# Decoded weights and half of the norm rows turned in 32x32 blocks on VectorE in place of TensorE

## What is computed

```python
x = x + attention(layernorm(x), ctx, ctx, mask, wq, wk, wv, wo)   # 32 query heads, 8 key heads, rope
x = x + (layernorm(x) @ w_l.T + bias)     # w_l[o, i] = lut4[o, 4-bit code of (o, i)]
```

## Time and profile before

| what | us |
|---|---|
| median of 3 runs (2350.05 to 2352.4) | 2351.77 |
| span of the profiled execution, first to last instruction | 2348.6 |
| stage A / B / C in it | 384.3 / 1781.9 / 182.4 |
| TensorE busy | 2330.7 |
| VectorE busy | 1690.5 |
| ScalarE busy | 1115.5 |

### The profile page before, as it was taken

One profiled execution on the slowest core, in us unless ns is written; L12 is line 12 of the kernel. 1 busy time (PEld: TensorE's weight loads), 2 busy tenths in 40 slices (PEclk: granted clock), 3 DMA queues, 4 the chain that ended last, 5 costly groups with the idle time before them and its releaser, 6 DMA issues.

```text
span 2348.6 us, 35132 instructions
## 1 busy us (share of the span) xinstructions
PE 2330.7 (99%) x11878; PEld 1989.3 (85%) x11878; DVE 1690.5 (72%) x3808; ACT 1115.5 (47%) x2469; POOL 570.1 (24%) x674
## 2 busy tenths in 40 slices
PE   9999999999999999999999999999999999999999
PEld 8999998788888888888888888888888888888787
DVE  7888777677776767777776767676777777776773
ACT  5555544555464646455544445444544444443110
POOL 1000001222232223232322232223323232322220
PEclk9999999999999999999999999999999999999999
DMA  7466558533344343434457633333333333335442
GB/s 258 159 199 213 190 177 299 170 109 117 115 133 120 109 127 111 129 107 128 117 162 238 209 104 115 90 112 109 112 93 113 105 100 111 107 93 185 122 142 81
DMA packets 330098, 328.26 MB, mean 140 GB/s; under 512 B 32448, under 2 KB 266176, under 8 KB 329920
## 3 DMA queue, kind: packets, MB, share of 16 engines
q1 hardware_dynamic: 294496, 309.88, 42.8%
q10 hardware_dynamic: 35424, 16.14, 2.6%
HBM read 181.73 MB, written 71.30 MB: 108 GB/s over the span
## 4 chain that ended last, share of the span: by engine, by line
PE 92%; DVE 3%; DMA 3%; ACT 1%; SPq 1%; issue 1%; POOL 0%; ACTq 0%; DVEq 0%
PE bank L829 28%; PE bank L915 28%; PE bank L845 7%; PE bank L886 7%; PE bank L783 7%; PE bank L955 7%; PE bank L760 7%; DMA small_split<-probs 1%; DMA k_scratch<-small_split 1%; SPq L615 0%; POOL probs L1930 0%; DMA small_split<-k_scratch 0%; DVE residual L1804 0%; PE bank L721 0%; PE bank L741 0%
## 5 line engine op out<-in xcount | busy, mean ns | idle before, releaser
L915 PE MATMUL bank<-weights_split,small_split 128*128 128x512 f32 x3072 | 741.0, 390 | 1.9 <-DVE small_split L1788 1.9
L829 PE MATMUL bank<-acts_split,weights_split 128*128 128x512 f32 (+1 forms) x3168 | 742.9, 384 | 0.0
L915 PEld LDWEIGHTS bank<-weights_split,small_split 128*128 128x128 f32 x3072 | 574.4, 188 | 121.6 <-DVE small_split L1788 3.2
L829 PEld LDWEIGHTS bank<-acts_split,weights_split 128*128 128x128 f32 x3168 | 575.1, 188 | 110.6
L1930 POOL TENSOR_SCALAR probs<-probs,row_numbers 128x256 f32<-128x256 f32 x512 | 359.3, 714 | 1192.9 <-DVE row_numbers L1774 1192.9
L1248 ACT ACTIVATE probs<-bank,row_numbers 128x256 f32<-128x256 f32 x512 | 238.1, 472 | 125.2 <-DVE row_numbers L1769 125.0
L1778 DVE STREAM_TRANSPOSE probs<-probs 128x512 f32<-128x512 f32 x250 | 177.7, 711 | 145.2 <-POOL probs L1930 145.2
L1922 POOL TENSOR_TENSOR rope_x<-rope_x,sin_t 128x512 f32<-128x512 f32 (+1 forms) x132 | 166.7, 1263 | 404.7 <-ACT rope_x L1221 404.5
L1763 DVE CUSTOM_DVE_ANT_0 bank<-bank,mask_tile 128x256 f32<-128x256 f32 x512 | 207.2, 447 | 64.5 <-PE bank L845 64.4
L1783 DVE TENSOR_TENSOR small_split<-small_split 128x512 fp32r<-128x512 f32 x250 | 178.8, 715 | 85.2 <-ACT small_split L1261 85.0
L845 PEld LDWEIGHTS bank<-small_split 128*128 128x128 f32 x1536 | 217.6, 190 | 23.0 <-DVE small_split L1743 1.6
(11 more groups left out here) (124 smaller groups left out, 2167.0 us busy)
## 6 DMA issues: line engine op xcount, KB each, us to landing
small_split<-probs SPq DMA_DIRECT2D x754, 64.0 KB, 2.2
raw<-in_L_xattn_wq SPq DMA_DIRECT2D x61, 512.0 KB, 3.8
raw<-in_L_xattn_wo SPq DMA_DIRECT2D x60, 512.0 KB, 3.8
k_scratch<-small_split SPq DMA_DIRECT2D x64, 256.0 KB, 2.3
v_scratch<-small_split SPq DMA_DIRECT2D x32, 512.0 KB, 2.9
x_scratch<-raw SPq DMA_DIRECT2D x64, 256.0 KB, 2.8
acts_split<-x_scratch SPq DMA_DIRECT2D x32, 512.0 KB, 5.0
mask_tile<-in_mask_BxSxS_ff SPq DMA_DIRECT2D x64, 256.0 KB, 3.0
```

What stands on the lines that cost most here:

```text
L829: last = pe.matmul(query_bank(j)[:, 0:wide], wq_s[:, h, c, a, :], xT[:, c, m, b * S:b * S + wide], start=c == 0 and i == 0, stop=c == C - ...
L915: last = pe.matmul(out_ps[part][:, :], o_s[:, a, u % 2 * S + t * P:u % 2 * S + (t + 1) * P], wo_s[:, h, m, n * BANK:(n + 1) * BANK], start ...
```

## The change

Weight tiles 0 to 7 and row tiles 0 to 7 are turned by VectorE, with two STREAM_TRANSPOSE instructions of 128x512 each, from SBUF into the same PSUM banks as before. They turn each 32x32 block in itself. To make that enough, they read every fourth number of a row (`block_order`), and four DMAs of 32 partitions by 1024 numbers each (`store_blocks`) lay the blocks in DRAM so that it holds the picture of SBUF, which is then loaded in whole stripes of 4 KB (rows) or 8 KB (weights) per partition. The layouts of `w4_s`, `xT` (rows 0 to 7, `xT_blocks`) and `wv_s` follow; the moving operand of the queries of the first half and of stage C is then 16 runs of 32 numbers, 1 KB apart, where it was one run of 512. HI and LO of a tile now use one buffer one after the other: HI of both halves, four stores, then LO in its place once these have landed, four stores. Row tile 8 stays on TensorE, as do tiles 9 to 15 in stage B.

The first tile of stage C multiplies column half 0 fully and then half 1, because the pieces of `w4_s` are now halves of columns and parts; the turning of row tile 1 stands within it. The queries of batches 0 and 4 wait for all eight pieces of their `xT` half before the first one, not pair by pair.

The core of the diff:

```diff
         wk_s = W[:, :].rearrange("p (c l n) -> p c l n", c=C, l=2)
-        wv_s = X[:, :].rearrange("p (c l n) -> p c l n", c=C, l=2)
+        wv_s = X[:, :].rearrange("p (h c l n) -> p h c l n", h=NN, c=C, l=2)
...
         xT = X[:, :].rearrange("p (c l n) -> p c l n", c=C, l=2)
+        xT_half = X[:, :].rearrange("p (h c l n) -> p h c l n", h=2, c=C, l=2)
+        xT_blocks = X[:, :].rearrange("p (h l m c t) -> p h l c m t", h=2, l=2, c=C, t=QUAD)
...
-        w4_s = W[:, :].rearrange("p (c l n) -> p c l n", c=C, l=2)
+        w4_s = W[:, :].rearrange("p (h l m c t) -> p h l c m t", h=NN, l=2, c=C, t=QUAD)
...
+        def weight_stage(tile, part):
+
+            if tile == NB - 1:
+                return acc[:, HT - 2 + part, :].bitcast(F32R)
+            return x_split_all if tile == NB - 2 else v_stage_all
+
+        def block_order(row, half):
+
+            return row.rearrange("p (c i m) -> p m c i", c=C, i=QUAD)[:, 2 * half:2 * half + 2]
...
+            def store_blocks(image, at, src, done):
+
+                for a in range(PARTS):
+                    sp.dma_start(image[:, at + a * S:at + (a + 1) * S], src[a * QUAD:(a + 1) * QUAD, :]).then_inc(done, 16)
+
             def store_row(e, j):
 
+                if e < HT:
+                    if j == HI:
+                        sp.wait_ge(x_hi, 2 * e + 2)
+                    else:
+                        sp.wait_ge(x_lo, 2 * e + 2)
+                    store_blocks(x_blocks, (e // REP * 2 + j) * REP * D + e % REP * D, raw, x_stored)
+                    return
...
-                def store_weights(tile, i):
-                    sp.wait_ge(stage_lo, STAGED // 2 + staged_count(tile, i))
-                    stage, stored = staging(tile, i)
-                    dst = w_scr.rearrange("p j k (t n) -> t j p k n", n=P)
-                    sp.dma_start(dst[tile, i - D0], stage.bitcast(F32).rearrange("p (k n) -> p k n", n=P)
-                                 ).then_inc(stored, 16)
+                def store_weights(tile, part):
+                    sp.wait_ge(w4_lo if part else w4_hi, 2 * tile + 2)
+                    store_blocks(w_scr, (tile // REP * 2 + part) * REP * D + tile % REP * D,
+                                 weight_stage(tile, part).bitcast(F32), w4_stored)
...
-            def turn_weights(tile):
-
-                pe.wait_ge(w4_ready, tile + 1)
-                pe.wait_ge(stage_lo, STAGED // 2 + tile * STAGED)
-                for c in range(C):
-                    done = pe.transpose(w4_ps[c // 4][:, (c % 4) * P:(c % 4 + 1) * P],
-                                        picks[0][:, c * P:(c + 1) * P], ident[:, :])
-                    if c % 4 == 3:
-                        done.then_inc(w4_tr, 1)
...
                 values(0)
-                if b in K_ROW:
+                if b in K_ROW and K_ROW[b] >= HT:
                     turn_row(K_ROW[b])
                 values(1)
                 values(2)
                 values(3)
-                if b in V_ROW:
-                    turn_row(V_ROW[b])
...
-                columns = [(n, c) for n in range(NN) for c in range(C)] if f == NT - 1 else [
-                    (n, c) for c in range(C) for n in range(NN)]
-                for n, c in columns:
-                    if f == 0 and n == 0:
-                        pe.wait_ge(w4_in[c], 16)
-                    for i, (a, m) in enumerate(PASSES):
-                        last = pe.matmul(out_ps[f % 2 * NN + n][:, :],
-                                         xT[:, c, a, f % HT * P:(f % HT + 1) * P],
-                                         w4_s[:, c, m, n * BANK:(n + 1) * BANK],
-                                         start=c == 0 and i == 0, stop=c == C - 1 and i == 2)
-                    if c == C - 1:
+                if f == 0:
+                    products = [(0, c, k) for c in range(C) for k in range(3)]
+                    products += [(1, c, k) for c in range(C) for k in (0, 2)] + [(1, c, 1) for c in range(C)]
+                elif f == NT - 1:
+                    products = [(n, c, k) for n in range(NN) for c in range(C) for k in range(3)]
+                else:
+                    products = [(n, c, k) for c in range(C) for n in range(NN) for k in range(3)]
+                ends = [max(at for at, product in enumerate(products) if product[0] == n) for n in range(NN)]
...
+                    if f == 0 and (n, c, k) == (1, C // 2 - 1, 2) and PE_ROWS > 1:
+                        turn_rows(1)
...
+            def blocks_high(e):
+
+                act.wait_ge(x_tr, 2 * e + 2)
+                act.wait_ge(x_stored, rows_stored(e))
+                for j in range(2):
+                    act.activation(x_split[:, j, :], x_ps[j][:, :], ACT.Copy).then_inc(x_hi, 1)
...
+                def weights_high(tile):
+                    act.wait_ge(w4_tr, 2 * tile + 2)
+                    if tile == NB - 2:
+                        act.wait_ge(x_stored, rows_stored(A_ROWS))
+                    elif tile < NB - 2:
+                        act.wait_ge(v_stored, 16 * (v_turn(tile, V2) + 2))
+                    for j in range(2):
+                        act.activation(weight_stage(tile, HI)[:, j * BANK:(j + 1) * BANK], w4_ps[j][:, :],
+                                       ACT.Copy).then_inc(w4_hi, 1)
...
+            def turn_row_blocks_early(e):
+
+                dve.wait_ge(row_ok, e + 1)
+                dve.wait_ge(x_lo, 2 * e)
+                for j in range(2):
+                    dve.transpose(x_ps[j][:, :], block_order(ln_row[:, :], j)).then_inc(x_tr, 1)
+
+            def blocks_low(e):
+
+                dve.wait_ge(x_hi, 2 * e + 2)
+                dve.wait_ge(x_stored, rows_stored(e) + 16 * PARTS)
+                for j in range(2):
+                    dve.tensor_tensor(x_split[:, j, :], x_ps[j][:, :], x_split[:, j, :].bitcast(F32),
+                                      ALU.subtract).then_inc(x_lo, 1)
...
+            def turn_weight_blocks(tile):
+
+                dve.wait_ge(w4_ready, tile + 1)
+                dve.wait_ge(w4_lo, 2 * tile)
+                for j in range(2):
+                    dve.transpose(w4_ps[j][:, :], block_order(picks[0], j)).then_inc(w4_tr, 1)
+
+            def weights_low(tile):
+
+                dve.wait_ge(w4_hi, 2 * tile + 2)
+                if tile < NB - 1:
+                    dve.wait_ge(w4_stored, 16 * PARTS * (2 * tile + 1))
+                for j in range(2):
+                    half = slice(j * BANK, (j + 1) * BANK)
+                    dve.tensor_tensor(weight_stage(tile, LO)[:, half], w4_ps[j][:, :],
+                                      weight_stage(tile, HI)[:, half].bitcast(F32), ALU.subtract).then_inc(w4_lo, 1)
...
-                    if g == TURN_AT[b]:
-                        weights_low(b - 1, D0)
+                    if g == TURN_AT[b] - 1:
+                        turn_weight_blocks(b - 1)
                     if g == SECOND_AT[b]:
-                        weights_low(b - 1, D1)
...
+                if b in K_ROW and K_ROW[b] < HT:
+                    turn_row_blocks_early(K_ROW[b])
                 values_low(V0)
...
+                if b in K_ROW and K_ROW[b] < HT:
+                    blocks_low(K_ROW[b])
+                elif b in K_ROW:
                     x_low(K_ROW[b], 1, x_ps[1])
...
                 values_low(V2)
                 for j in range(4):
                     context_low(4 * (b + 1), j)
+                if b in V_ROW:
+                    turn_row_blocks_early(V_ROW[b])
```

181 lines of the change are left out of this document (83 added, 98 removed).

## The result

| | median us | runs | ratio to before, 95% interval |
|---|---|---|---|
| before | 2351.23 | 4 (2350.05 to 2352.4) | |
| changed kernel | 2394.47 | 4 (2392.12 to 2396.2) | 1.0179 (1.0165 to 1.0193) |

What follows compares the result with a forecast made beforehand. TensorE bounds the kernel, unless VectorE is late. Span 2348.6 - 3.6 (batches 1 to 7) + 0.3 (stage B) + 1.8 (stage C) = 2347.1; median 3.2 above: 2350.3 us; bounds 2347 to 2355.5, wider range 2342 to 2358.

Steps and rivals of the forecast that it cites:

- Bound and places: Whole kernel: TensorE bounds it; it would wait for VectorE ahead of V2 in batch 1 and behind V3 in 2 to 4.
- The image wait in batch 1: Batch 1: VectorE waits 1.2 us for the HI image's four stores, since HI and LO share a buffer.
- Stage C's step: Stage C: row tile 1 is turned behind 32 matmuls, not 24, and nothing covers the delay: +1.8 us.
- I take no cost: First-half queries and stage C: reading 16 runs of 32 costs TensorE nothing, from 394 ns against 390.
- I take no surcharge: VectorE's added transposes: reading every fourth number costs nothing extra, so a pair takes about 1.25 us.
- rival 4: First-half queries and stage C: short runs make 2304 matmuls 5 ns longer each, +11.5 us, 2361.8; chance 0.05.
- rival 3: VectorE's transposes at 16-byte steps: a pair takes 2.4 us, not 1.25; 12 pass on 1.15 each, +13.8, 2364; chance 0.06.
- the batches' terms: Stage A, batches 1 to 7: turns saved on TensorE less VectorE's lateness, together -3.6 us.
- term +1.4: Batch 1: V2 starts at 92.45 in place of 91.08, 1.4 us longer although 1.6 of TensorE work has gone.
- terms +1.1, -1.25, -1.25: Batches 2 to 4: batch 2 longer by the second row tile's later load and chain; 3 and 4 save 2.4 us, lose some.
- terms -3.6 together: Batches 5 to 7: mostly turns saved on TensorE, -1.2, -0.8 and -1.6 us.
- term +0.3: Stage B's start: all eight `xT` loads must land before the first queries; later idle time takes up most of it.

Runs made afterwards that it cites:

- e8_quarter: Kernel before, with 14 of the 16 turns that the change removes making two of their eight matmuls (results meaningless): 2347.28 us against 2352.29, ratio 0.9985.
- e12_quarter_again: The kernel of e8_quarter run once more, for a second trace: 2350.38 us.
- e4_plain: Changed kernel, with first-half queries and stage C reading one run of 512 and the 32 transposes reading one run (results meaningless): 2363.36 us.
- e1_reads: Kernel before, with stage C's moving operand read in another pattern of run length and step in most row tiles (results meaningless): 2368.41 us.
- e11_steps: Kernel before, with more moving-operand patterns in stage C and extra VectorE transposes and a copy at longer steps: 2359.08 us.
- e6_own_low: The kernel of e4_plain, with LO parts written to a spare buffer, so VectorE doesn't wait for the HI image (results meaningless): 2360.83 us.
- e10_turn12: Kernel before, complete, with row tile 1 turned behind the first 12 matmuls of stage C in place of 24: 2348.04 us against 2350.85, ratio 0.9986.
- e13_fill: Changed kernel, complete, with 57 more unread matmuls that keep TensorE busy in stage A's waits: 2392.94 us.
- e9_turn24: The kernel of e4_plain, with row tile 1 in stage C turned behind 24 matmuls again, not 32: 2363.97 us.
- cross of four kernels: Changed kernel with short runs or one run of 512, transposes reading every fourth number or one run: 2394.47, 2376.07, 2384.98, 2363.36 us.
- e5_turn_only: Changed kernel, with only the 32 transposes reading one run of 512 in place of every fourth number (results meaningless): 2384.98 us.

## Why the prediction was wrong, by its steps

**Bound and places: right.** TensorE waits where the text said: V2 of batch 1 behind V0's LO part, key 0 of batches 3 to 5 behind the context's. The turn is worth about what I took, 0.79 us: 14 times three quarters of a turn gave 8.3 us in stage A of e8_quarter and 6.6 in e12_quarter_again (0.63 each). The image wait in batch 1 was 1.14 us for 1.2. Stage C's step cost what it should: the wait was 4.03 us in e4_plain where it had been 2.28, 1.75 more for the forecast 1.8 (and the clock behind it came on top).

**The first step that failed: two terms of the sum put at nothing, "I take no cost" for the short runs and "I take no surcharge" for the transposes.** They stood as rivals 4 and 3, at chances of 0.05 and 0.06. Both were true at once and cost about 31 us, most of the 36 by which the time lies above my range. In both I let one row decide that didn't show the operation.

- *Short runs (rival 4).* The earlier trace rows showed 394 ns for runs of 64 against 390, and I explained the 4 ns away by what stands around line 886. By e1_reads runs of 64 cost 3 ns and runs of 32 ten to eleven. The row had the warning in it; the nearest pattern in the trace was twice as long as the new one, which is a reason to extrapolate beyond it. The rival's price should have been 4 to 10 ns on 2304 matmuls, 9 to 23 us, with a chance near one half. And the order of magnitude was at hand: a turn saves 0.79 us once, a turned weight tile is read by 96 matmul-shares (768 / 8) and a row tile by 192 (1536 / 8), so at 9 to 11 ns they cost 1.1 and 1.7 us each. The change could not gain on TensorE itself.
- *The transposes' step (rival 3).* I held L1459, 1264 ns for 1024 numbers at 128 bytes, against the contiguous transpose, 1246, and read "no surcharge". These are two operations. The copy in e11_steps with a step of 128 bytes takes 1.12 us per 512 against 0.69 for one run. L1459 is a TENSOR_SCALAR, and the one of that kind and size that reads one run in the kernel before (L1562, on integers) takes 819:

```profile
L1459 DVE TENSOR_SCALAR ln_row<-residual,row_numbers 128x1024 f32<-128x1024 f32 x16 | 20.3, 1267 | 27.7 <-DMA raw<-ln_row 27.6
...
L1562 DVE TENSOR_SCALAR residual<-residual,probs 128x1024 int32<-128x1024 int32 x64 | 50.8, 819 | 1.1 <-ACT residual L1113 1.1
```

So the surcharge was most likely in the row that I took as proof of its absence. The rule of the Trainium skill (page "SBUF — State Buffer", section "Door 1: The DMA port swizzle"), which spoke against the change, deserved more than 0.06. The surcharge was 0.7 to 0.8 us per pair, not the 1.15 of the rival, and it cost 11 us.

**The second: the batches' terms, even at my own prices.** In e4_plain batches 1 to 7 took 8.1 us more than in the kernel before (391.3 - 54.0 against 384.3 - 55.1), where the sum had -3.6. Batch 0, which had no term, was 1.1 shorter.

- *Batch 1*, term +1.4, measured +3.4 (50.28 for 46.89). V2 waited 3.56 us for 2.95, and 48 matmuls behind it took 12.63 us for 11.07: the clock, which no term had.
- *Batches 2 to 4*, terms +1.1, -1.25, -1.25, measured +3.2, +1.7 and +2.6. The row chain is longer than I made it. I took 10.0 us from the arrival of the second row to the context's LO part, less 1.2 us of waits that I thought gone. They are not. In e4_plain these steps of batch 2 take 10.0 us (144.11 to 154.13), and the load goes out 35.3 us into the batch for my 34.4: 1.2 + 0.9, the 2.1 by which the term was short. With the slower transposes it is more. In batch 2 of the changed kernel (ScalarE):

```profile
147.41 1.06 ACT L1025 ACTIVATE ln_row<-ln_row 128x1024 f32<-128x1024 f32 x1 [3.54 <-DMA ln_row<-in_x]
...
152.93 0.60 ACT L1040 ACTIVATE bank<-ln_row 128x512 f32<-128x512 f32 x1 [2.85 <-DVE raw L1445]
```

The load goes out 36.8 us into the batch, at 142.79, and takes 4.6 us, as I took it. But the squares of the second row are written into the banks of the first, whose LO part must be done; that stands behind V1's LO part, V1's HI copy stands on ScalarE behind the mean of the row that comes late, and then the LO part waits for its image too. From 147.41 to the context's LO at 158.45 it is 11.0 us, not 8.8. e6_own_low, without the image wait, gave 7.7 us of stage A back in its trace.

- *Batches 5 to 7*, terms -3.6 together, measured -2.8.

**The clock.** The forecast had no term for it, though the kernel before shows it: behind the 2.28 us of the earlier trace rows the clock is 0.86 for 12.6 us. I read the clock where TensorE was busy and not behind its waits. e10_turn12 shows the price, 1.8 us for that wait, where the clock falls; in stage A e13_fill shows 2.6 us at most, no more than the spread between traces, since VectorE's lateness covers the rest.

**Stage B**, term +0.3. The term has one wait too small. In e4_plain the first queries that need the eight loads of `xT` stand 3.40 us for them (1.92 in the changed kernel), not 0.3:

```profile
419.54 4.42 PE L846 MATMUL bank<-acts_split,weights_split 128*128 128x512 f32 x12 [3.40 <-DMA acts_split<-x_blocks]
```

But the waits behind it shrink: the 1.20, 0.86 and 2.97 us of the kernel before become one of 0.29. Twelve query matmuls start 49.1 us into stage B in the kernel before (433.42), and the same ones 48.9 us into it in e4_plain (440.16). The 2.4 us by which its stage B is longer come later, and they lie within the 4.8 us between e4_plain and e9_turn24. What sets that spread is open. The one place looked at closely is that of the 3.47 us in e12_quarter_again: from 1285 to 1345 us the block DMAs that ScalarE issues there take 4.4 us from issue to landing (median of 8), against 2.4 (of 9) in the kernel before, from 1293 to 1353.

In the order of size: short runs 20 us, transposes 11, batches and clock at my own prices about 10, stages B and C 3 (together the 44 from 2350.3 to 2394.5). The first two come out of the cross of four kernels; the split of the other 13 goes by single traces and is an estimate.

## What to carry to other kernels

Before moving work off the bound engine, count how often the bound engine reads the result in its new layout: here 96 and 192 reads at 9 to 11 ns cost more than the one turn that was saved. When a price is taken from the nearest row, take one of the same operation or divide out the difference, and when the new case lies beyond the row (runs of 32 beyond 64), extrapolate. Look at the clock right behind every idle time of TensorE: a wait of 2.3 us cost 4.1 in the kernel before and 2.3 in e12_quarter_again. Before a difference of some us in one stage of one trace is explained, take two traces of the same code.

## What the runs showed of the hardware that I had not expected

- TensorE's moving operand: one run of 512 is started every 227 ns (busy time per matmul); 16 runs of 32 at 1 KB cost 9 to 11 ns more, every other split that was tried 3 ns or more, 32x288 only 3 ns where 32x256, 32x320 and 32x272 cost 10 to 14 (by the mean duration), runs of 8 57. I have no rule for it.
- VectorE reads at a step of 16 bytes and more at 1.07 to 1.23 us per 512 numbers, at 4 or 8 bytes at 0.69 to 0.73, in copies and transposes alike.
- The granted clock often fell from 2.4 to 1.2 GHz behind an idle time of TensorE, for up to some 6 us, and did so for one length and not for another that was as long: it fell behind 1.81 us in e6_own_low, 1.97 in e4_plain, 2.28 in the kernel before and 3.71 in the changed kernel, and not behind 2.26 in the changed kernel and in e12_quarter_again, 2.38 in e6_own_low, 2.97 in stage B of the kernel before or 3.70 in e5_turn_only. Where other waits cover it, giving it back is worth less than its own size (2.6 us at most of 6.6).
- Where stage A was 8.3 and 6.6 us shorter, stage B was 4.7 and 8.1 us longer, in part at the place where bulk stores and loads meet the block DMAs, while five traces with both stages as in the kernel before differ by 1.6 and 2.0 us. The path is open.
